# Row maxima of an attention kernel: split by GpSimd, turned by TensorE onto their own two partitions, and read four slots later

## The reference

```python
x = x + attn(layernorm(x))          # 16 heads, HEAD_DIM 16, S 2048
x = x + ffn(layernorm(x))           # ternary weights, d_ff 1024

# attn:
scores = einsum('bhqd,bhkd->bhqk', q, k) / sqrt(D)
mask = einsum('hnqk,hn->hqk', dp[:, :, None, None] ** abs(t[:, None] - t[None, :]), softmax(mix))
probs = softmax(scores * mask[None], axis=-1)
out = einsum('bhqk,bhkd->bhqd', probs, v)
```

## Time and profile before

| what | value |
|---|---|
| median of 3 runs | 1913.11 us (1912.32 to 1914.3) |
| profiled execution: time | 1910.07 us |
| profiled execution: span | 1908.3 us |
| mean granted TensorE clock | 0.95 |
| busy: PE, DVE, ACT, POOL | 1705.1, 1527.7, 1427.4, 912.7 us |
| DMA traffic | 300.03 MB, 157 GB/s |

### The profile page before, as it was taken

How to read it: one execution, slowest core, us unless ns; L and a number is a source line. 1 busy time by engine, 2 the same in 40 slices (tenths; PEclk the granted TensorE clock), 3 DMA queues, 4 the chain that set the end, 5 groups by cost and what they waited for, 6 DMA issues and landing times.

```text
span 1908.3 us, 31293 instructions
## 1 busy us (share of the span) xinstructions
PE 1705.1 (89%) x10834; PEld 589.1 (31%) x10834; DVE 1527.7 (80%) x2638; ACT 1427.4 (75%) x2669; POOL 912.7 (48%) x915
## 2 busy tenths in 40 slices
PE   7836899998989899989898989899999999999998
PEld 5401222222222222223232222222222222224666
DVE  5766888787878787878787888888887878796885
ACT  6524878787878787878787878778787878787665
POOL 6733637363636454555545464636373636343010
PEclk9867999999999999999999999999999999999999
DMA  6967574756565665748484757575747575562640
GB/s 206 331 205 187 149 169 126 179 136 170 144 159 146 151 160 146 178 120 198 116 192 131 177 141 173 148 168 144 174 130 183 129 178 143 139 186 59 159 125 34
DMA packets 195217, 300.03 MB, mean 157 GB/s; under 512 B 92114, under 2 KB 115538, under 8 KB 184914
## 3 DMA queue, kind: packets, MB, share of 16 engines
q1 hardware_dynamic: 188980, 296.85, 61.1%
q10 hardware_dynamic: 6080, 1.19, 0.4%
HBM read 152.18 MB, written 42.99 MB: 102 GB/s over the span
## 4 chain that ended last, share of the span: by engine, by line
PE 59%; DVE 15%; issue 9%; DMA 5%; SPq 3%; ACT 2%; POOL 1%; DVEq 0%; ACTq 0%
PE tile L1664 21%; PE ring L1679 20%; PE ring L1633 11%; DVE masked L1425 5%; DMA late<-max_rows 4%; DVE unseen L1425 4%; DVE max_parts L1443 3%; PE tile L1661 2%; PE ring L1749 2%; SPq L233 1%; ACT late L1379 1%; PE tile L1731 1%; SPq L202 1%; DVE qk L1514 1%; DMA raw_scratch<-late 1%
## 5 line engine op out<-in xcount | busy, mean ns | idle before, releaser
L1379 ACT ACTIVATE late<-tile 128x512 f32<-128x512 f32 x2048 | 1107.6, 604 | 321.1 <-PE tile L1664 219.5
L1425 DVE CUSTOM_DVE_ANT_0 masked<-ring,mask 128x1024 f32<-128x1024 f32 x512 | 625.0, 1221 | 180.7 <-PE ring L1633 158.1
L1425 DVE CUSTOM_DVE_ANT_0 unseen<-ring,mask 128x1024 bf16<-128x1024 f32 x512 | 625.0, 1221 | 100.1 <-PE ring L1633 100.1
L1679 PE MATMUL ring<-late,v_ones 128*32 128x512 f32 x4096 | 569.7, 629 | 0.1
L1207 POOL COPY diag<-masked 128x128 f32<-128x128 f32 x512 | 149.0, 291 | 780.3 <-DVE part_max L1425 769.6
L1633 PE MATMUL ring<-k_raw,q_raw 64*128 64x512 f16 x2048 | 351.6, 397 | 88.9 <-DVE part_max L1425 76.7
L1664 PE MATMUL tile<-late 98*128 98x512 f16 (+2 forms) x1280 | 330.0, 345 | 62.2 <-issue 48.0
L1664 PE MATMUL tile<-q_stack,k_stack 98*128 98x512 f16 (+2 forms) x1280 | 316.8, 334 | 11.6 <-ACT late L1379 8.5
L289 POOL TENSOR_TENSOR decayed<-qk,table_in 128x1024 f32<-128x1024 f32 x120 | 284.1, 2367 | 2.4 <-DMA table_in<-table_scratch 2.3
L308 POOL TENSOR_TENSOR lo<-decayed,hi 128x1024 f16<-128x1024 f32 x120 | 256.3, 2136 | 0.0
L1664 PEld LDWEIGHTS tile<-late 98*128 98x128 f16 x1280 | 101.7, 99 | 389.7 <-ACT late L1379 239.7
(11 more groups left out here) (148 smaller groups left out, 1049.1 us busy)
## 6 DMA issues: line engine op xcount, KB each, us to landing
mask<-mask_row_scratch SPq DMA_DIRECT2D x128, 496.0 KB, 7.5
table_in<-table_scratch SPq DMA_DIRECT2D x64, 256.0 KB, 8.4
q_raw<-raw_scratch SPq DMA_DIRECT2D x128, 128.0 KB
k_stack<-hi SPq DMA_DIRECT2D x64, 256.0 KB, 4.0
q_stack<-hi SPq DMA_DIRECT2D x128, 128.0 KB, 3.8
late<-hi SPq DMA_DIRECT2D x64, 256.0 KB, 8.7
late<-hi SPq DMA_DIRECT2D x128, 128.0 KB, 8.0
out_scratch<-heads_out SPq DMA_DIRECT2D x64, 256.0 KB, 6.2
```

Of the source, the lines that this page charges most:

```text
L1379: nc.scalar.activation(probs[:, (2 * s + x // 2) % 4, x % 2 * 512:(x % 2 + 1) * 512], tile[:, n % TILE_BANKS], ACT.Exp, scale=1.0 / (SCALE ...
L1425: nc.vector.tensor_tensor_reduce(out=masked[:, b % 2] if diagonal else unseen[:], in0=pair, in1=factor, scale=1.0, scalar=-3.0e38, op0=ALU ...
L1679: last = nc.tensor.matmul(acc[row:row + ROWS], v_ones[h][:, t % BLOCKS], probs[:, t % 4, qt * 512:(qt + 1) * 512], start=(j % UNIT_SLOTS = ...
```

## The change

VectorE no longer splits the maxima. GpSimd does it with three operations on 128x8 (`max_neg`, then the high and the low part), without the four repetitions, after the diagonal copy of slot 3 (RED_SLOT is now 3). In slot 4 TensorE turns the two parts block by block, eight transposes of 128x2, onto partitions 96 and 97 of a `tile` bank. ScalarE copies the bank (2x1024) straight into level 0 of `q_stack`; a DMA spreads it from there to levels 1 to 3. Key blocks are taken in the order that `key_block` gives: those of the other half first, those of the own half from slot 4 of the unit (NEAR_SLOT). At a unit's start TensorE waits for the copy and for the loads of levels 0 and 1; at slot 4 for the loads of levels 2 and 3, the DMA of the rows and the diagonal, which GpSimd now finishes in slot 7 (DIAG_SLOT). The tables of products, rests and casts are shifted, the first product from slot 2 to slot 4. On SP the load of the pair after next moves ahead of the store of the third unit's sums and of the loads of levels 2 and 3, and waits for the last product in place of the last rest.

```diff
-RED_SLOT, TURN_SLOT = 4, 5
+RED_SLOT = (UNIT_SLOTS - 1 - LEAD) % UNIT_SLOTS
+TURN_SLOT = RED_SLOT + 1
+NEAR_SLOT = UNIT_SLOTS // 2
+DIAG_SLOT = UNIT_SLOTS - 1
...
+def key_block(t, half):
+    return (t + (1 - half) * UNIT_SLOTS) % BLOCKS
...
-        pool_slot = {2: ("product", 0), 4: ("product", 1), 7: ("rest", 0), 8: ("product", 2), 10: ("rest", 1),
-                     11: ("product", 3), 12: ("rest", 2), 14: ("product", 4), 15: ("rest", 3), 16: ("product", 5),
-                     18: ("rest", 4), 19: ("product", 6), 20: ("rest", 5), 22: ("product", 7), 24: ("rest", 6),
+        pool_slot = {4: ("product", 0), 5: ("product", 1), 8: ("rest", 0), 9: ("product", 2), 10: ("rest", 1),
+                     12: ("product", 3), 13: ("rest", 2), 14: ("product", 4), 16: ("rest", 3), 17: ("product", 5),
+                     18: ("rest", 4), 20: ("product", 6), 21: ("rest", 5), 22: ("product", 7), 24: ("rest", 6),
                      26: ("rest", 7)}
-        cast_slot = {5: (0, 0), 6: (0, 1), 7: (1, 0), 8: (1, 1), 9: (2, 0), 10: (2, 1), 12: (3, 0), 13: (3, 1),
-                     15: (4, 0), 16: (4, 1), 17: (5, 0), 18: (5, 1), 20: (6, 0), 21: (6, 1), 23: (7, 0), 24: (7, 1)}
+        cast_slot = {5: (0, 0), 6: (0, 1), 7: (1, 0), 9: (1, 1), 10: (2, 0), 11: (2, 1), 13: (3, 0), 14: (3, 1),
+                     15: (4, 0), 17: (4, 1), 18: (5, 0), 19: (5, 1), 21: (6, 0), 22: (6, 1), 23: (7, 0), 25: (7, 1)}
...
+                if i + 2 < STEPS:
+                    sp.wait_ge(builder.decayed_ready, CHUNKS * (i + 2))
+                    builder.load(sp, i + 2)
                 store_out(i, 2)
                 if more:
                     sp.wait_ge(lo_ready, CHUNKS * (i + 2))
                     load_k(0, 1)
                     load_q(0, 0, 1)
                     load_q(0, 1, 1)
-                if i + 2 < STEPS:
-                    builder.load(sp, i + 2)
...
+            def split_max(par, slot, o, count):
+                hi, lo = max_parts[:, :, 0], max_parts[:, :, 1]
+                pool.wait_ge(max_ready, count)
...
+                nc.gpsimd.tensor_tensor(max_neg[:], row_max[:, par], down_unit[:].broadcast_to([P, UNIT_SLOTS]), ALU.mult
+                                        ).then_inc(neg_ready, 1)
+                pool.wait_ge(neg_ready, count)
+                nc.gpsimd.tensor_copy(hi, max_neg[:]).then_inc(max_hi, 1)
+                pool.wait_ge(max_hi, count)
+                nc.gpsimd.tensor_tensor(lo, max_neg[:], hi, ALU.subtract).then_inc(parts_ready, 1)
...
-                nc.scalar.copy(max_rows[:], tile[0:MAXROWS * LO_ROWS, n % TILE_BANKS, 0:P // 2].bitcast(F16)
-                               ).then_inc(exp_done, 1)
+                nc.scalar.copy(q_stack[h][STACK:STACK + MAXROWS, half, 0],
+                               tile[STACK:STACK + MAXROWS, n % TILE_BANKS].bitcast(F16)).then_inc(exp_done, 1)
...
-                act.dma_start(q_stack[h][STACK:STACK + MAXROWS, half], max_rows[:]).then_inc(rows_in, QUADS)
+                act.dma_start(q_stack[h][STACK:STACK + MAXROWS, half, 1:DEPTH],
+                              q_stack[h][STACK:STACK + MAXROWS, half, 0].unsqueeze(1).broadcast_to([MAXROWS, DEPTH - 1, HALF])
+                              ).then_inc(rows_in, QUADS)
...
-            def split_max(par, count):
-                hi, lo = max_parts[:, 0], max_parts[:, 1]
-                row = row_max[:, par].unsqueeze(1).broadcast_to([P, DEPTH, UNIT_SLOTS])
...
-                nc.vector.scalar_tensor_tensor(out=hi, in0=row, scalar=-1.0 / MAXUNIT,
-                                               in1=zero[:].unsqueeze(2).broadcast_to([P, DEPTH, UNIT_SLOTS]),
-                                               op0=ALU.mult, op1=ALU.add).then_inc(max_hi, 1)
-                dve.wait_ge(max_hi, count)
-                nc.vector.scalar_tensor_tensor(out=lo, in0=row, scalar=-1.0 / MAXUNIT, in1=hi, op0=ALU.mult,
-                                               op1=ALU.subtract).then_inc(parts_ready, 1)
...
-                nc.tensor.transpose(tile[0:MAXROWS * LO_ROWS, n % TILE_BANKS, 0:P // 2].bitcast(F16),
-                                    max_parts[:].rearrange("p r l b -> p (r l b)"), keep["ident16"][:]).then_inc(tile_full, 1)
+                for b in range(UNIT_SLOTS):
+                    last = nc.tensor.transpose(tile[STACK:STACK + MAXROWS, n % TILE_BANKS, b * P // 2:(b + 1) * P // 2].bitcast(F16),
+                                               max_parts[:, b], keep["ident16"][:])
+                last.then_inc(tile_full, 1)
...
                     if s % UNIT_SLOTS == 0:
                         u = s // UNIT_SLOTS
-                        for done in (*(k_in[u // 2] if u % 2 == 0 else ()), *q_in[u // 2][u % 2]):
+                        pe.wait_ge(exp_done, last_turn(TURN_SLOT + s, o) + TILE_BANKS + 1)
+                        for done in (k_in[u // 2][0], q_in[u // 2][u % 2][0]):
                             pe.wait_ge(done, PART_DMAS * QUADS * (i + 1))
...
+                    if s % UNIT_SLOTS == NEAR_SLOT:
+                        u = s // UNIT_SLOTS
+                        for done in (k_in[u // 2][1], q_in[u // 2][u % 2][1]):
+                            pe.wait_ge(done, PART_DMAS * QUADS * (i + 1))
                         pe.wait_ge(rows_in, QUADS * (UNITS * i + u + 1))
                         pe.wait_ge(diag_ready, UNITS * i + u + 2)
```

More of the change, by code:

```diff
@@ L838, in items_done, with last_turn @@
     return RING_STEP * o + ring_item(slot, ITEMS - 1) + AHEAD_ITEMS + 1
+def key_block(t, half):
+    return (t + (1 - half) * UNIT_SLOTS) % BLOCKS
+def last_turn(slot, o):
+    if slot < 0 or (slot == TURN_SLOT and o == 0):
+        return 0
+    return turn_item(slot - UNIT_SLOTS, o) if slot >= UNIT_SLOTS else turn_item(slot + SLOTS - UNIT_SLOTS, o - 1)
 def score_parts(block, side):
@@ L1214, in diag_minus_max @@
                                         ALU.subtract).then_inc(diag_ready, 1)
+            def split_max(par, slot, o, count):
+                hi, lo = max_parts[:, :, 0], max_parts[:, :, 1]
+                pool.wait_ge(max_ready, count)
+                if count == 1:
+                    pool.wait_ge(unit_ready, 1)
+                if count > 1:
+                    pool.wait_ge(exp_done, last_turn(slot + 1, o) + TILE_BANKS + 1)
+                nc.gpsimd.tensor_tensor(max_neg[:], row_max[:, par], down_unit[:].broadcast_to([P, UNIT_SLOTS]), ALU.mult
[4 more added lines that the diff above has]
+                nc.gpsimd.tensor_tensor(lo, max_neg[:], hi, ALU.subtract).then_inc(parts_ready, 1)
             def add_out_bias(g):
@@ L1270, in _ @@
                 keep_diag(s, 0)
-                if s == TURN_SLOT - UNIT_SLOTS:
+                if s == RED_SLOT - UNIT_SLOTS:
+                    split_max(0, s, 0, 1)
+                if s == DIAG_SLOT - UNIT_SLOTS:
                     diag_minus_max(0, 0, 1)
@@ L1277, in step @@
                     u = s // UNIT_SLOTS + 1
-                    if s % UNIT_SLOTS == TURN_SLOT and (more or u < UNITS):
+                    if s % UNIT_SLOTS == RED_SLOT and (more or u < UNITS):
+                        split_max(u % 2, s, o, UNITS * i + u + 1)
+                    if s % UNIT_SLOTS == DIAG_SLOT and (more or u < UNITS):
                         diag_minus_max((u // 2) % 2, u % 2, UNITS * i + u + 1)
@@ L1559, in _ @@
                 max_block(s, 0)
-                if s % UNIT_SLOTS == RED_SLOT and s + LEAD >= UNIT_SLOTS:
+                if s == RED_SLOT - UNIT_SLOTS:
                     finish_max(0, items_done(s, 0), None)
-                    split_max(0, 1)
             def step(i, o, more):
@@ L1645, in turn_max @@
                 pe.wait_ge(parts_ready, count)
-                nc.tensor.transpose(tile[0:MAXROWS * LO_ROWS, n % TILE_BANKS, 0:P // 2].bitcast(F16),
-                                    max_parts[:].rearrange("p r l b -> p (r l b)"), keep["ident16"][:]).then_inc(tile_full, 1)
+                for b in range(UNIT_SLOTS):
+                    last = nc.tensor.transpose(tile[STACK:STACK + MAXROWS, n % TILE_BANKS, b * P // 2:(b + 1) * P // 2].bitcast(F16),
+                                               max_parts[:, b], keep["ident16"][:])
+                last.then_inc(tile_full, 1)
             def scores(t, o, halves=range(2)):
-                u, kb = t // BLOCKS, t % BLOCKS
+                u = t // BLOCKS
                 h, half = u // 2, u % 2
+                kb = key_block(t % BLOCKS, half)
                 for x in halves:
@@ L1678, in products @@
                         row = (2 * par + qt) * ROWS
-                        last = nc.tensor.matmul(acc[row:row + ROWS], v_ones[h][:, t % BLOCKS],
+                        last = nc.tensor.matmul(acc[row:row + ROWS], v_ones[h][:, key_block(t % BLOCKS, u % 2)],
                                                 probs[:, t % 4, qt * 512:(qt + 1) * 512],
@@ L1780, in _ @@
                 max_scores(s, range(ITEMS), 0)
```

(2 more changed lines are left out.)

33 lines of the change are left out of this document (14 added, 19 removed).

## The result

The changed kernel takes 1891.34 us (median of 3 runs, 1889.26 to 1899.36) against 1913.11: a ratio of 0.9886, with a 95% interval of 0.984 to 0.9932. It is faster by about 1%, where 144 us (7.5%) were forecast, and outside the range of 1745 to 1822. The profiled execution has a span of 1897.5 us and a time of 1899.36.

The account below looks back on a forecast made before the run. TensorE was taken as the bound: 87.6 us a step plus 1.6 and 0.8 gives 90.0 against 99.7. That saves 136 us over 14 steps, plus 4 and 4, 144 in all: 1913 becomes 1769 us, range 1745 to 1822.

Parts of the forecast that it names:

- SP's loads of the next pair's rows and tables: SP's queue: moved ahead of nine k and q loads, which land within about 10 us, hidden by 24; priced at nothing.
- loads collide: Rival on SP's queue: tables delay the nine loads by some 3 us per step, 48 us, giving 1817; chance 0.06.
- TensorE is the bound where nothing disturbs it: Main loop: TensorE's work at 2.4 GHz is 87.6 of a 99.7 us step; the rest is idle time and slow clock.
- the sum of 90.0 us a step: Main loop: 87.6 us of TensorE work, 1.6 for turns and 0.8 kept back, saving 9.7 us in each of 14 steps.
- Split to GpSimd: Splitting the maxima: VectorE loses two instructions per unit, GpSimd gains three of 0.27 us, 0.8 us per unit, and keeps up.
- The transposes waited 0.5 us for it in the whole run; the margin: Between split and turn: 2.36 us available against about 1.4 needed, leaving 1.0 us of cover before TensorE would wait.
- GpSimd's small operations: Rival at the split: VectorE blocks hold all three operations, the split takes 3.7 us longer, 171 us, 1940; chance 0.04.
- Turn: TensorE's turning slot: seven more transposes per unit at 0.057 us each, 1.6 us a step.
- ScalarE's copy: Copy to level 0 after the turn: 1.006 us for 0.258, 0.75 more per unit, hidden by ScalarE's spare time.
- the 0.8 us of friction: Every step: 0.2 us per unit kept back because the copy and the split sit in the same slot.
- Row DMA needed four slots later: DMA of levels 1 to 3: read 21 us after issue against 11.3 at the slowest, so both of its waits go.
- Sum outside the 14 steps: First and last step: a gain of 4 us each, on top of 136 us, making 144 together.

Follow-up runs that it names:

- e3: Changed kernel with the max pass's raw rows loaded with the dimension of 16 outermost, so all DMA engines share each load; 1746.63 us, ratio 0.9095.
- e5: Kernel before the change with only the raw rows of the max pass spread over more DMA engines; 1794.26 us, ratio 0.937.
- e1: Changed kernel with SP's old order: the load of the pair after next last again, behind the nine k and q loads; 1892.48 us, ratio 0.9846.
- e6: e3's kernel with the split given back to VectorE as two 128x8 instructions, none on GpSimd; 1745.75 us, ratio 0.9114.
- e10: e3's kernel with each turn's eight transposes done twice; 1775.57 us.
- e7: e3's kernel with TensorE waiting at a unit's start, not slot 4, for the rows' DMA and the loads of levels 2 and 3; 1752.51 us, ratio 0.9156.
- e4: Changed kernel with both e1's old order on SP and e3's spread raw rows; 1746.68 us, ratio 0.9094.

## Why the prediction was wrong

The step that failed is the one on **SP's loads of the next pair's rows and tables**, "priced at nothing": the nine loads behind them were to be out within 7 us and to land within about 10. They were out in 10.1 us (937.25 to 947.35), and the last pieces of their three groups landed after 21 to 27. The sum had no term for what was already queued at that place: eight raw loads, on two DMA engines, from 19 us earlier on. In the kernel before the nine loads went out from 953.63 on, after the masks' last arrival at 952.6, and landed within 5 us. The change sends them out while those two engines are at work on the raw loads, until 945.2, and then on the masks, until 956.1.

The symptom is the one that the rival *loads collide* named (chance 0.06, 3 us a step), but the cause is another: in e3 the tables stand in front of the nine loads just as in the change, and these land within 12 us, about as priced. The wait costs 99.24 - 90.06 = 9.2 us a step. TensorE is busy for 1279.69 of 1389.30 us in the loop after, 91.4 us of a step against 89.07 in e3: 2.3 us of the 9.2 are the slow clock behind the wait, the other 6.9 are idle time. In 14 steps this is 129 us. The profiled spans of the change as given and of e3 are 151.6 us apart; nearly all of the other 23 lie in the first step (105.2 us against 90.1, counted from the first values product of a step to that of the next) and ahead of it (154.6 against 146.6). That 1769 + 129 = 1898 comes within 7 us of the measured time is luck: two errors outside the 14 steps, of about 22 us each, cancel. The stretch for these numbers:

```profile
222.00:1611.30 1389.30, 1279.69 (x8515) 403.75 (x8514) 1074.52 (x1848) 1145.63 (x2129) 764.08 (x897) 0.95 0.66 156
```

Behind it stands a reading that went wrong already in the kernel before. I took the 11.3 us of the row DMA as the duration of this transfer. That the wait belongs to it was right (its last arrival comes at 943.0, and TensorE goes on at 943.23), but the length was a symptom: e5 removes these waits without touching the DMA. The 10.16 us of a table load weren't: the tables' median landing is 8.4 us before and 8.5 in e5. I took 0.64 as the load of the DMA engines, a mean over 16 engines of which two had a queue of their own, and a mean over the step: from 930 to 956 us of the kernel after, where the late loads are issued, the share is about 1. With the cause left in place, the change only moved the wait: from the rows in slot 0 to the k and q loads in slot 4, and with e1 to a cast in slot 5.

The other steps, one by one:

- *TensorE is the bound where nothing disturbs it; the sum of 90.0 us a step*: right, 90.06 in e3.
- *Split to GpSimd*: 0.204 + 0.196 + 0.209 = 0.61 us a unit for 0.8. The transposes waited 0.5 us for it in the whole run; the margin held, and GpSimd's small operations were not held. But e6 shows that the change of engine was not what mattered.
- *Turn*: 39.4 / 64 = 0.62 us at full clock, as worked out (0.219 + 7 x 0.057); e10 confirms the price of a further transpose.
- *ScalarE's copy*: 1.005 us as forecast. It lies on the chain of e3, but the step has about the 0.8 us of friction that I left for it (90.06 - 89.07 = 1.0).
- *Row DMA needed four slots later*: its wait is gone, as forecast. But this relief is worth 6 us once the loads are spread (e7), not the larger part of the forecast gain.
- *Sum outside the 14 steps*: mis-sized, to the other side. e3 is 22 us under the forecast although its step agrees. Counted from the first values product of a step to that of the next, the part ahead of it takes 156.9 us before and 146.6 in e3, the first step 111.9 and 90.1, the last 91.4 and 95.6. So the forecast's 4 us for the first step were 22, its 4 for the last were a loss of 4, and 10 ahead of the loop had no term. e5 has 150.8 and 94.1: 6 of the 10 and 18 of the 22 come with e3's own edit, not with the change. (The 1.7 us of slow clock in the term for the last step stand on no row; the wait in the kernel after costs 2.3 in each step.)

The gain of 167 us from the old kernel to e3 is thus made of 119 for spreading the raw loads, and 48 for the change on top of that (1794.26 against 1745.75 in e6, on one chip). Without the spread, the change shows 22. Which part of the 48 the shifted tables alone would bring in the old kernel wasn't tried. The best versions, e3, e4 and e6, lie within 1 us of one another at 1746.

## What to carry to other kernels

A transfer that takes longer than its bytes ask for may be waiting behind another transfer: before moving its consumer, look for what was issued in the 20 us ahead of it, and for a load whose outermost dimension is small. A list of issues in which one load has no landing, or a semaphore with fewer than 16 arrivals for a load, is a hint of it, and no more than that: the maxima's DMA has three arrivals in e3 too, and nothing waits for it there. And an edit that moves a wait is priced at nothing only with the landing times of the queue at its new place, not with those of a quiet stretch.

## What the runs showed of the hardware

- Loads with an outermost dimension of 2 gave 3 semaphore arrivals each. Eight of them (768 KB) delayed two of the 16 arrivals of each load that SP issued behind them, so that loads issued 7 to 28 us after the first of them were complete only 21 to 27 us after their issue. The mean busy share of the DMA engines in the loop was 0.66 with that delay and 0.68 without it (e3). The same bytes with a dimension of 16 outermost gave 16 arrivals, landed in 2.4 to 2.7 us, and took 145 us off the changed kernel (1891.3 to 1746.6) and 119 off the old one.
- A DMA on another queue was late with them: the maxima's DMA is issued by ScalarE, has three arrivals itself, and landed after 6.5 us in the median before and 3.1 when SP's raw loads were spread (e5).
- VectorE operations of 0.19 us were held for 1.34, 2.03 and 1.95 us, three in each step of e5, in slots where GpSimd runs long operations. They cost some 4 us a step by the estimate above, nearly the 4.8 us by which they were longer.
- Eight further transposes of 128x2 cost 0.45 us in a slot in which TensorE sets the pace (e10).
